# Row-by-row indirect DMAs of a graph network: straight-line GpSimd code that reads whole tables

## Chip, cores, metric

One Trainium2 chip, one core. The metric is the device time of one execution in microseconds (us).

## What is computed

Two graph layers on 6250 nodes of 128 features and 100000 edges (src, dst), each with a residual and a layer norm:

```python
# layer 0: attention along the edges, softmax over the edges of one src
scores = sum(q[src] * k[dest], -1) / sqrt(D) + attention_mask
weights = softmax of scores within each src
out = segment_sum(v[src] * weights, dest) @ Wo.T + bo
x = layernorm(x + out)
# layer 1: a two-layer MLP on each edge, summed by src, then an MLP on the nodes
h = silu(concat([x[src], x[dst], edge_attr_2]) @ eW1 + eb1)
agg = segment_sum(silu(h @ eW2 + eb2), src)
x = layernorm(x + silu(concat([x, agg]) @ nW1 + nb1) @ nW2 + nb2)
```

## The kernel before

An edge is a record of 16 floats: 8 attention biases, 2 attributes, dst, the lane of src within its window of 128 nodes, its id. The program runs through stages, each a block with one instruction stream per engine and a barrier at its end.

**Placing** (`place_and_project`, L362). The 784 columns of 128 records are taken 8 at a time (98 groups, `PG`). VectorE, TensorE and ScalarE work out for each record the row of `records_dram` where it belongs, sorted by window. VectorE ends a group with the row indices `row_idx` (L499), in a buffer of two groups; it first waits until the DMAs of two groups ago have landed. GpSimd copies each column of records into `rec_out` (L627) and scatters it with an indirect DMA, 128 rows of 64 bytes (L640); the copy of a column is issued ahead of the DMA of the column before. 784 copies, 784 DMAs. Beside it q, k and v are projected, 49 windows.

**Loading** (`load_records`, L688). The sorted records, 832 columns, come back into SBUF as `records`, in 7 pieces; VectorE takes the lanes out of each (L717).

**Scoring** (`score`, L742). 104 groups of 8 columns. GpSimd casts each column's whole record to integers (`sc_idx`, L789), and then gathers 128 rows of k by its dst (L800): 832 casts, 832 DMAs, in a ring of 4 groups. TensorE makes the q rows with one-hot matrices; VectorE multiplies and sums.

**Softmax**, **weighing** (`weigh`, L1063 on; 832 scatters that add, L1106) and the **middle** of the network follow.

**Edges** (`edges`, L1630). 208 groups of 4 columns. VectorE casts the dst of a group to `ed_idx` (L1694, three groups ahead) once that ring slot's gather before has landed; GpSimd gathers 4 times 128 rows of `b_rows_dram` (L1685) in a ring of 4 groups; TensorE sums window rows, attributes and gathered rows in PSUM (`ps_z`), and a SiLU, a second matmul, a SiLU and a one-hot matmul follow; VectorE adds the sums to `vals` (L1719). **Finale**: the MLP on nodes.

GpSimd's three loops are written with `each_pair` and `each_group`: some groups at either end as straight-line code, the rest in a hardware loop of 2 or 4 groups. The order on every queue is the program's order; nothing schedules it.

Of the kernel before, what the change touches and what calls it, by code (L numbers as in the profile page):

```python
# [26 lines left out]
F32 = mybir.dt.float32  # L27
BF16 = mybir.dt.bfloat16
I32 = mybir.dt.int32

P = 128
# [8 lines left out]
ET = 784  # L40
LASTE = E - (P - 1) * ET
G = 4
# [3 lines left out]
R = 16  # L46
# [12 lines left out]
PG = 8  # L59
IT = ET // PG  # L60
RF = NT // 16

# [299 lines left out]
def place_and_project(c, e, a):  # L362
# [6 lines left out]
             "place_counted place_slots masked slot slot_int slot_tile slot_scaled slot_lane slot_chunk slot_line row_index rec_slot")  # L369
    (s_ohl, s_ohw, s_tr, s_lt, s_gram, s_gm, s_tab, s_hist, s_slots, s_msk, s_red, s_int, s_tile, s_mul, s_lane, s_chunk,  # L370
     s_line, s_idx, s_rec) = semaphores(nc, c.sems, names)
    s_sent = semaphores(nc, c.stack, "records_sent0 records_sent1")
# [3 lines left out]
    with ExitStack() as t:  # L376
# [15 lines left out]
        idx = sb("row_idx", [P, 2, PG], I32)  # L392
        out = sb("rec_out", [P, 2, PG, R], F32)
# [12 lines left out]
        with nc.Block() as block:  # L406
# [28 lines left out]
            def _(dve):  # L435
# [37 lines left out]
                def finish(i, b):  # L473
# [24 lines left out]
                    wait_count(dve, s_sent[b], 16 * PG * i)  # L498
                    dve.scalar_tensor_tensor(out=idx[:, b, :], in0=chunk[:, :], scalar=-float(NT - 1), in1=line[:, :],  # L499
# [122 lines left out]
            @block.gpsimd  # L622
            def _(pool):
                pool.wait_ge(c.s_rfill, 16 * (NT // RF))

                def record(g, b, j):
                    pool.tensor_copy(out[:, b, j, :], e.rec[:, bass.ds(g * PG + j, 1), :].rearrange("p t r -> p (t r)")  # L627
                                     ).then_inc(s_rec, 1)

                def send(i, b):  # L630
                    g = 2 * i + b
                    wait_count(pool, s_sent[b], 16 * PG * i)
                    record(g, b, 0)
                    pool.wait_ge(s_idx, g + 1)
                    for j in range(PG):
                        if j + 1 < PG:
                            record(g, b, j + 1)
                        pool.wait_ge(s_rec, PG * g + j + 1)
                        pool.sem_inc(s_turn, 1)
                        pool.indirect_dma_start(  # L640
                            c.rec_rows, bass.IndirectOffsetOnAxis(ap=idx[:, b, j:j + 1], axis=0),
                            out[:, b, j, :], None, bounds_check=SLOTS - 1, oob_is_err=False).then_inc(s_sent[b], 16)
                each_pair(pool, send)
                for b in range(2):
                    pool.wait_ge(s_sent[b], 16 * PG * (IT // 2))
# [42 lines left out]
def load_records(c):  # L688
# [6 lines left out]
    s_l, s_t, s_row, s_out = semaphores(nc, c.sems, "lanes_taken lanes_turned lane_rows lanes_out")  # L695
# [46 lines left out]
def score(c):  # L742

    nc = c.nc
    names = ("sc_onehot_t sc_q sc_index sc_prod sc_dot sc_score sc_line sc_kept sc_ids sc_ids_t "
             "sc_ids_kept sc_ids_shift sc_steps")
    (s_oht, s_q, s_idx, s_prod, s_dot, s_sc, s_line, s_kept, s_ids, s_idt, s_idk, s_shift,
# [9 lines left out]
    with ExitStack() as t:  # L757
# [3 lines left out]
        idx = sb("sc_idx", [P, RING, SG, R], I32)  # L761
# [10 lines left out]
        with nc.Block() as block:  # L772
# [8 lines left out]
            def _(pool):  # L781
# [4 lines left out]
                def index(g, r, k):  # L786
                    if k == 0:
                        wait_count(pool, s_k[r], (g - r) * (16 * SG // RING))
                    pool.tensor_copy(idx[:, r, k, :], c.rec[:, bass.ds(g * SG + k, 1), :].rearrange("p t r -> p (t r)")  # L789
                                     ).then_inc(s_idx, 1)  # L790

                def gather(g, r):
                    wait_count(pool, s_prod, g - RING + 1)
                    for k in range(SG):
                        ahead, slot, there = (g, r, True) if k + 1 < SG else group_at(g, r, 1, NS)
# [1309 lines left out]
```

## Time and profile before

| what | us |
|---|---|
| median of 3 runs (5821.47 to 5829.13) | 5822.44 |
| span of the profiled execution, first to last instruction | 5485.4 |
| placing, first to last of GpSimd's DMAs | 160.33 to 1328.12 |
| scoring, the same | 1362.57 to 2517.35 |
| edges, the same | 4350.84 to 5412.71 |

The profile carries no time of its own for the profiled execution, only its span. It lies 337.0 us under the median of the runs; that much is spent before the first and after the last instruction of the record. Engines: PE is TensorE, PEld its weight load, DVE VectorE, ACT ScalarE, POOL GpSimd, SP SyncE. An indirect DMA on POOL (DMA_INDIRECT) is busy while GpSimd makes its descriptors; the data moves after that on the DMA engines. "Idle" before an instruction is the time its engine did nothing just before it, with what ended that; "issue" is time in which nothing that the profile shows was waited for.

### The profile page before, as it was taken

The numbers are of one execution on the slowest core, as the hardware profiler recorded it, in microseconds if no ns is written. First come the engines' busy times: TensorE is split into PE (matmuls) and PEld (weight loads), VectorE is DVE, ScalarE is ACT, GpSimd is POOL, SyncE is SP. The second block draws the span as 40 slices with busy tenths as digits, with TensorE's granted clock in tenths as the row PEclk, the third lists the DMA queues.
The fourth block names the chain that finished last, engine by engine and source line by source line (L and its number), as shares of the span: only waits on it lengthen the run. The fifth ranks groups of instructions, "written<-read, shape, count | busy, mean of one in ns | idle before, by whom it ended". The sixth has DMA issues, their size and how long they took to land. (4 is left out here: it accounts for less than half of the span.)

```text
span 5485.4 us, 85482 instructions
## 1 busy us (share of the span) xinstructions
PE 2866.4 (52%) x21791; PEld 2562.0 (47%) x21792; DVE 2423.9 (44%) x6521; ACT 779.2 (14%) x1649; POOL 4120.0 (75%) x5002
## 2 busy tenths in 40 slices
PE   6444444442333333331565666666653577778776
PEld 5333333331333333331455555555553466677765
DVE  7655555552333333336533333333333644444445
ACT  0111111110000000000111111111111322222222
POOL 1688888886888888883588888888886377777773
PEclk9666666665555555555787778787786799999999
DMA  2300000001222222220243444444445433333333
GB/s 85 110 11 11 10 11 11 11 10 68 72 72 71 69 72 70 70 71 21 24 35 35 35 35 35 35 35 35 35 35 94 120 78 77 77 78 76 78 76 82
DMA packets 301449, 293.46 MB, mean 53 GB/s; under 512 B 62976, under 2 KB 240570, under 8 KB 300377
## 3 DMA queue, kind: packets, MB, share of 16 engines
q0 software_dynamic: 201376, 176.66, 20.7%
q1 hardware_dynamic: 100024, 116.22, 7.2%
q8 instruction: 22, 0.36, 0.0%
q14 instruction: 27, 0.22, 0.0%
HBM read 198.74 MB, written 93.92 MB: 53 GB/s over the span
## 5 line engine op out<-in xcount | busy, mean ns | idle before, releaser
L1106 POOL DMA_INDIRECT sums_dram<-we_merged_rows,we_idx x832 | 1289.7, 1550 | 385.3 <-issue 204.6
L1685 POOL DMA_INDIRECT ed_bg<-b_rows_dram,ed_idx x832 | 808.7, 972 | 262.5 <-issue 240.7
L800 POOL DMA_INDIRECT sc_k<-k_rows_dram,sc_idx x832 | 827.1, 994 | 145.3 <-POOL sc_idx L789 130.4
L640 POOL DMA_INDIRECT records_dram<-rec_out,row_idx x784 | 779.2, 994 | 207.9 <-POOL rec_out L627 164.4
L900 PE MATMUL ps_q<-tab,sc_oht 128*128 x1664 | 386.5, 426 | 740.8 <-DVE sc_oht L813 740.8
L900 PEld LDWEIGHTS ps_q<-tab,sc_oht 128*128 128x128 f32 x1664 | 358.8, 327 | 772.3 <-issue 772.3
L1257 PE MATMUL ps_merged<-we_rows,we_same_dst 128*128 128x129 f32 x1664 | 337.7, 366 | 585.2 <-issue 428.9
L1257 PEld LDWEIGHTS ps_merged<-we_rows,we_same_dst 128*128 128x128 f32 x1664 | 288.9, 261 | 620.9 <-issue 611.4
L1159 DVE SCALAR_TENSOR_TENSOR we_firsts<-we_merged_rows,lane_unmark,two_marks 128x4 f32<-128x4 f32 x208 | 46.3, 222 | 1012.6 <-ACT we_merged_rows L1202 1012.6
L828 DVE TENSOR_TENSOR sc_prods<-ps_q,sc_k 128x1024 f32<-128x1024 f32 x104 | 127.3, 1224 | 745.3 <-DMA sc_k<-k_rows_dram,sc_idx 745.3
L1719 DVE TENSOR_TENSOR vals<-vals,ps_ed_s 128x128 f32 x832 | 238.9, 287 | 391.8 <-PE ps_ed_s L1816 296.7
L1795 PE MATMUL ps_z<-ident,ed_bg 128*128 128x128 f32 x832 | 250.2, 301 | 243.7 <-DMA ed_bg<-b_rows_dram,ed_idx 243.5
L591 PE MATMUL ps_table<-place_ohw,place_oh 128*128 128x400 bf16 (+7 forms) x784 | 167.4, 392 | 323.2 <-DVE place_ohw L216 323.2
L1237 PE MATMUL ps_dst_row<-ident,we_dsts 128*128 128x128 f32 x1664 | 329.7, 365 | 0.0
L1237 PEld LDWEIGHTS ps_dst_row<-ident,we_dsts 128*128 128x128 f32 x1664 | 315.2, 282 | 0.0
L1202 ACT ACTIVATE we_merged_rows<-ps_merged 128x516 f32<-128x516 f32 x208 | 125.0, 601 | 1283.1 <-DMA sums_dram<-we_merged_rows,we_idx 1268.8
L1792 PE MATMUL ps_z<-ed_oht,tab 128*128 128x128 bf16 x2496 | 306.1, 226 | 0.0
L591 PEld LDWEIGHTS ps_table<-place_ohw,place_oh 128*128 128x128 bf16 x784 | 113.6, 163 | 381.8 <-issue 329.6
L627 POOL COPY rec_out<-records 128x16 f32 (+1 forms) x784 | 182.6, 243 | 129.3 <-POOLq L276 112.1
L1247 PE MATMUL ps_v<-value_tab,we_oht 128*128 x1664 | 275.1, 317 | 0.1
L572 PE MATMUL ps_place_t<-identb,place_oh 128*128 128x128 bf16 x784 | 92.0, 283 | 313.4 <-DVE place_oh L222 313.4
L1795 PEld LDWEIGHTS ps_z<-ident,ed_bg 128*128 128x128 f32 x832 | 121.6, 146 | 276.9 <-DMA ed_bg<-b_rows_dram,ed_idx 276.6
(307 smaller groups left out, 6534.6 us busy)
## 6 DMA issues: line engine op xcount, KB each, us to landing
sc_lane_rows<-lanes_dram SPq DMA_DIRECT2D x104, 256.0 KB, 3.4
ed_lane_rows<-lanes_dram SPq DMA_DIRECT2D x104, 256.0 KB
sc_k<-k_rows_dram,sc_idx POOLq DMA_INDIRECT x832, 2.5
sums_dram<-we_merged_rows,we_idx POOLq DMA_INDIRECT x832, 3.3
ed_bg<-b_rows_dram,ed_idx POOLq DMA_INDIRECT x832
sums_dram<-zero_rows SPq DMA_DIRECT2D x20, 640.0 KB, 8.7
records_dram<-rec_out,row_idx POOLq DMA_INDIRECT x784
mi_rows<-sums_dram SPq DMA_DIRECT2D x48, 256.0 KB, 4.5
```

Source lines behind the costliest of these rows:

```text
L591: ins = pe.matmul(table[:, k:PG, :], ohl[:, b, :, k], ohw[:, b, k, :].unsqueeze(1).to_broadcast([P, PG - k, WC]), start=(k == 0), stop=Tru ...
L640: pool.indirect_dma_start(c.rec_rows, bass.IndirectOffsetOnAxis(ap=idx[:, b, j:j + 1], axis=0), out[:, b, j, :], None, bounds_check=SLOTS ...
L800: pool.indirect_dma_start(kg[:, r, k * F:(k + 1) * F], None, c.k_dram[:, :], bass.IndirectOffsetOnAxis(ap=idx[:, r, k, C_DST:C_DST + 1], a ...
L900: ins = pe.matmul(psq[b][:, k * F:(k + 1) * F], oht[:, b, k, :], c.qtab[:, bass.ds(win[k] * F, F)], start=True, stop=True)
L1106: pool.indirect_dma_start(c.acc_dram[k][:, :], bass.IndirectOffsetOnAxis(ap=idx[:, r, k:k + 1], axis=0), rows[:, r, k, 0:F], None, compute ...
L1237: ins = pe.matmul(psd[:, k * P:(k + 1) * P], dst[:, r, k:k + 1].to_broadcast([P, P]), c.ident[:, :], start=True, stop=True)
L1247: ins = pe.matmul(psv[b][:, k * F:(k + 1) * F], oht[:, b, k, :], c.vtab[:, bass.ds(win[k] * F, F)], start=True, stop=True)
L1257: ins = pe.matmul(merged[b][:, k, 0:F + 1], same[:, b, k, :], con[:, b, k, :], start=True, stop=True)
L1685: pool.indirect_dma_start(bg[:, r, k * F:(k + 1) * F], None, c.b_dram[:, :], bass.IndirectOffsetOnAxis(ap=idx[:, r, k:k + 1], axis=0)).the ...
L1719: dve.tensor_tensor(acc, acc, pss[r % 2][:, k * P:(k + 1) * P], ALU.add).then_inc(s_add, 1)
L1792: pe.matmul(z, c.tab[:, j, bass.ds(win[k] * F, F)], oht[:, r, k, :], start=False, stop=False)
L1795: ins = pe.matmul(z, bg[:, r, k * F:(k + 1) * F], c.ident[:, :], start=False, stop=True, is_transpose=True)
```

## The change

GpSimd's three streams become straight-line code without loops, one DMA per column. In placing the DMA reads its 128 records straight from `records` (no `rec_out`, no copy), and the indices from a table of all 784 columns; VectorE no longer waits before it writes indices, and GpSimd waits for its own DMAs of four groups ago (`AHEAD`). The table `dst_index` of all 832 columns is filled in `load_records` by seven more casts on VectorE; scoring and edges take their indices from it (no `sc_idx`, no `ed_idx`, no casts in the stages). In edges the one-hot `ed_ohf` moves onto the records' memory to make room, and VectorE runs two groups ahead in place of three.

```diff
 place_and_project
-        idx = sb("row_idx", [P, 2, PG], I32)
-        out = sb("rec_out", [P, 2, PG, R], F32)
+        idx = sb("row_idx", [P, ET], I32)
...
-                    wait_count(dve, s_sent[b], 16 * PG * i)
-                    dve.scalar_tensor_tensor(out=idx[:, b, :], in0=chunk[:, :], scalar=-float(NT - 1), in1=line[:, :],
+                    dve.scalar_tensor_tensor(out=idx[:, bass.ds(g * PG, PG)], in0=chunk[:, :], scalar=-float(NT - 1), in1=line[:, :],
...
-                def record(g, b, j):
-                    pool.tensor_copy(out[:, b, j, :], e.rec[:, bass.ds(g * PG + j, 1), :].rearrange("p t r -> p (t r)")
-                                     ).then_inc(s_rec, 1)
-                def send(i, b):
-                    g = 2 * i + b
-                    wait_count(pool, s_sent[b], 16 * PG * i)
-                    record(g, b, 0)
-                    pool.wait_ge(s_idx, g + 1)
-                    for j in range(PG):
-                        if j + 1 < PG:
-                            record(g, b, j + 1)
-                        pool.wait_ge(s_rec, PG * g + j + 1)
...
+                for g in range(IT):
+                    pool.wait_ge(s_idx, g + 1)
+                    wait_count(pool, s_sent[g % AHEAD], 16 * PG * (g // AHEAD))
+                    pool.sem_inc(s_turn, 1)
+                    for t in range(g * PG, (g + 1) * PG):
+                        pool.indirect_dma_start(
+                            c.rec_rows, bass.IndirectOffsetOnAxis(ap=idx[:, t:t + 1], axis=0),
+                            e.rec[:, t, :], None, bounds_check=SLOTS - 1, oob_is_err=False).then_inc(s_sent[g % AHEAD], 16)
 load_records
+                    dve.tensor_copy(c.didx[:, t0:t0 + n], c.rec[:, t0:t0 + n, C_DST]).then_inc(s_di, 1)
 score
-                    pool.tensor_copy(idx[:, r, k, :], c.rec[:, bass.ds(g * SG + k, 1), :].rearrange("p t r -> p (t r)")
-                                     ).then_inc(s_idx, 1)
...
+                for g in range(NS):
+                    r = g % RING
                     wait_count(pool, s_prod, g - RING + 1)
+                    pool.sem_inc(s_turn, 1)
                     for k in range(SG):
+                        t = g * SG + k
                         pool.indirect_dma_start(kg[:, r, k * F:(k + 1) * F], None, c.k_dram[:, :],
-                                                bass.IndirectOffsetOnAxis(ap=idx[:, r, k, C_DST:C_DST + 1], axis=0)
+                                                bass.IndirectOffsetOnAxis(ap=c.didx[:, t:t + 1], axis=0)
                                                 ).then_inc(s_k[r], 16)
 edges
-        ohf = sb("ed_ohf", [P, RING, G, P], F32)
+        ohf = c.rec[:, 0:RING * G * P // R, :].rearrange("p t r -> p (t r)").rearrange("p (b k n) -> p b k n", b=RING, k=G)
...
-                def gather(g, r):
-                    pool.wait_ge(s_idx, g + 1)
+                for g in range(NG):
+                    r = g % RING
                     wait_count(pool, s_z, g - RING + 1)
                     pool.sem_inc(s_turn, 1)
                     for k in range(G):
+                        t = g * G + k
                         pool.indirect_dma_start(bg[:, r, k * F:(k + 1) * F], None, c.b_dram[:, :],
-                                                bass.IndirectOffsetOnAxis(ap=idx[:, r, k:k + 1], axis=0)
+                                                bass.IndirectOffsetOnAxis(ap=c.didx[:, t:t + 1], axis=0)
                                                 ).then_inc(s_b[r], 16)
...
-                def index(g, r):
-                    wait_count(dve, s_b[r], (g - r) * (16 * G // RING))
-                    dve.tensor_copy(idx[:, r, :], c.rec[:, bass.ds(g * G, G), C_DST]).then_inc(s_idx, 1)
...
-                    for by, work in ((3, index), (2, front), (0, by_edges), (-3, back)):
+                    for by, work in ((2, front), (0, by_edges), (-3, back)):
...
-                each_group(dve, step, lead=3, lag=3, rings=2)
+                each_group(dve, step, lead=2, lag=3, rings=2)
```

How GpSimd's queue stands in placing, before; one group of 8 columns in the loop, up to the next group's first copy. A row is one instruction, or xN of a kind; `waits` names the semaphores it waits for (`rec_slot` is the copy's, `records_sent0` and `1` the DMAs').

```order
L627 ISA [waits records_sent0]
L627 COPY rec_out<-records 128x16
L634 REGISTER_ALU
L627 ISA [waits row_index]
L627 COPY rec_out<-records 128x16
L640 DMA records_dram<-rec_out,row_idx 106496x16 [waits rec_slot]
L627 ISA
L627 COPY rec_out<-records 128x16
L640 DMA records_dram<-rec_out,row_idx 106496x16 [waits rec_slot]
```

And of the change, two groups of 8:

```order
L630 DMA records_dram<-records,row_idx 106496x16 [waits row_index,records_sent0]
L630 DMA records_dram<-records,row_idx 106496x16 x7
L630 DMA records_dram<-records,row_idx 106496x16 [waits row_index,records_sent1]
L630 DMA records_dram<-records,row_idx 106496x16 x7
```

Every copy between two DMAs is gone, and one DMA in eight waits for anything. Scoring, before, on the same queue:

```order
L800 DMA sc_k<-k_rows_dram,sc_idx 128x128 [waits sc_index]
L789 CAST sc_idx<-records 128x16
L800 DMA sc_k<-k_rows_dram,sc_idx 128x128 [waits sc_index]
```

And of the change:

```order
L781 DMA sc_k<-k_rows_dram,dst_index 128x128 [waits sc_prod]
L781 DMA sc_k<-k_rows_dram,dst_index 128x128 x7
```

The cast ahead of each gather is gone; the wait for the product of four groups ago stays, once in a group.

## Rows read from the trace of the kernel before

**Rows 1.** the page of the whole program: busy time, share and instructions of each engine

```profile
PE 2866.4 (52%) x21791; PEld 2562.0 (47%) x21792; DVE 2423.9 (44%) x6521; ACT 779.2 (14%) x1649; POOL 4120.0 (75%) x5002
```

**Rows 2.** busy time by stage: placing, scoring, edges. Columns stand in the first line

```profile
core 0: us, PE busy (x) PEld busy (x) DVE busy (x) ACT busy (x) POOL busy (x), PEclk, DMA share, GB/s
159.00:1328.00 1169.00, 478.41 (x4779) 376.88 (x4779) 629.68 (x1649) 128.33 (x243) 958.24 (x1567) 0.62 0.07 19
1361.00:2518.00 1157.00, 405.39 (x1766) 373.66 (x1766) 409.22 (x766) 33.16 (x152) 1007.78 (x1667) 0.58 0.28 71
4351.00:5413.00 1062.00, 819.70 (x7844) 738.37 (x7845) 487.42 (x1643) 282.37 (x621) 808.50 (x832) 0.97 0.32 77
```

**Rows 3.** groups by line on GpSimd: line, operation, count | busy us, mean ns | idle

```profile
L800 POOL DMA_INDIRECT sc_k<-k_rows_dram,sc_idx x832 | 827.1, 994 | 145.3 <-POOL sc_idx L789 130.4 <-issue 15.0
L1685 POOL DMA_INDIRECT ed_bg<-b_rows_dram,ed_idx x832 | 808.7, 972 | 262.5 <-issue 240.7 <-DVE ed_idx L1694 17.5 <-PE ps_z L1795 4.3
L640 POOL DMA_INDIRECT records_dram<-rec_out,row_idx x784 | 779.2, 994 | 207.9 <-POOL rec_out L627 164.4 <-issue 43.5
L627 POOL COPY rec_out<-records 128x16 f32 (+1 forms) x784 | 182.6, 243 | 129.3 <-POOLq L276 112.1 <-DVE row_idx L499 16.4
L789 POOL CAST sc_idx<-records 128x16 int32 (+1 forms) x832 | 181.0, 218 | 3.2
```

**Rows 4.** GpSimd in order of time, placing: start us, us, instruction [idle before <-releaser]

```profile
160.33 1.34 POOL L640 DMA_INDIRECT records_dram<-rec_out,row_idx  x1 [0.69 <-POOL rec_out L627]
...
604.80 0.21 POOL L627 COPY rec_out<-records 128x16 f32 x1
605.17 0.98 POOL L640 DMA_INDIRECT records_dram<-rec_out,row_idx  x1 [0.16 <-POOL rec_out L627]
...
613.21 0.97 POOL L640 DMA_INDIRECT records_dram<-rec_out,row_idx  x1 [0.30 <-issue]
...
1327.15 0.97 POOL L640 DMA_INDIRECT records_dram<-rec_out,row_idx  x1 [0.30 <-issue]
```

**Rows 5.** GpSimd in order of time, scoring

```profile
1362.57 1.01 POOL L800 DMA_INDIRECT sc_k<-k_rows_dram,sc_idx  x1 [0.77 <-POOL sc_idx L789]
...
2515.15 0.96 POOL L800 DMA_INDIRECT sc_k<-k_rows_dram,sc_idx  x1 [0.16 <-POOL sc_idx L789]
2516.41 0.94 POOL L800 DMA_INDIRECT sc_k<-k_rows_dram,sc_idx  x1 [0.30 <-issue]
```

**Rows 6.** GpSimd in order of time, edges

```profile
4341.48 0.12 POOL L1678 MEMSET ed_attrs<- 128x12 bf16 x1
4350.84 1.22 POOL L1685 DMA_INDIRECT ed_bg<-b_rows_dram,ed_idx  x1 [9.24 <-DVE ed_idx L1694]
...
4400.26 0.95 POOL L1685 DMA_INDIRECT ed_bg<-b_rows_dram,ed_idx  x1 [0.30 <-PE ps_z L1795]
...
5411.77 0.94 POOL L1685 DMA_INDIRECT ed_bg<-b_rows_dram,ed_idx  x1 [0.30 <-issue]
```

**Rows 7.** VectorE in order of time, placing

```profile
173.61 0.17 DVE L499 SCALAR_TENSOR_TENSOR row_idx<-slot_chunk_i,slot_line_f 128x8 int32<-128x8 int32 x1
...
180.28 0.17 DVE L499 SCALAR_TENSOR_TENSOR row_idx<-slot_chunk_i,slot_line_f 128x8 int32<-128x8 int32 x1
...
603.92 0.17 DVE L499 SCALAR_TENSOR_TENSOR row_idx<-slot_chunk_i,slot_line_f 128x8 int32<-128x8 int32 x1 [4.56 <-DMA records_dram<-rec_out,row_idx]
```

**Rows 8.** the scatter's line alone: count, duration ns min/median/max, first and last start

```profile
L640 POOL DMA_INDIRECT records_dram<-rec_out,row_idx x784: 966/977/1402, 160.3 to 1327.1; - x196
```

**Rows 9.** waits in edges, 4400 to 5350 us: us in total, times, longest us

```profile
PE ps_z L1795 <- DMA ed_bg<-b_rows_dram,ed_idx: 212.3, 161, 2.4
```

**Rows 10.** VectorE in order of time, loading of the records

```profile
1346.76 0.27 DVE L717 CAST lanes<-records 128x128 bf16<-128x128 f32 x1 [2.23 <-DMA records<-records_dram]
```

**Rows 11.** the page, DMA queues that carry instructions: packets, MB, share of 16 engines

```profile
q8 instruction: 22, 0.36, 0.0%
q14 instruction: 27, 0.22, 0.0%
```

More of the change, by code:

```diff
@@ L61 @@
 RF = NT // 16
+AHEAD = 4
 class Ctx:
@@ L368, in place_and_project @@
     names = ("place_onehot_n place_onehot_w place_turned place_onehot_t place_gram place_earlier place_table_kept "
-             "place_counted place_slots masked slot slot_int slot_tile slot_scaled slot_lane slot_chunk slot_line row_index rec_slot")
+             "place_counted place_slots masked slot slot_int slot_tile slot_scaled slot_lane slot_chunk slot_line row_index")
     (s_ohl, s_ohw, s_tr, s_lt, s_gram, s_gm, s_tab, s_hist, s_slots, s_msk, s_red, s_int, s_tile, s_mul, s_lane, s_chunk,
-     s_line, s_idx, s_rec) = semaphores(nc, c.sems, names)
-    s_sent = semaphores(nc, c.stack, "records_sent0 records_sent1")
+     s_line, s_idx) = semaphores(nc, c.sems, names)
+    s_sent = semaphores(nc, c.stack, " ".join(f"records_sent{n}" for n in range(AHEAD)))
     (s_turn,) = semaphores(nc, c.sems, "scatter_turn")
@@ L624, in _ @@
                 pool.wait_ge(c.s_rfill, 16 * (NT // RF))
[L626 to L645 removed]
+                for g in range(IT):
+                    pool.wait_ge(s_idx, g + 1)
+                    wait_count(pool, s_sent[g % AHEAD], 16 * PG * (g // AHEAD))
+                    pool.sem_inc(s_turn, 1)
+                    for t in range(g * PG, (g + 1) * PG):
+                        pool.indirect_dma_start(
+                            c.rec_rows, bass.IndirectOffsetOnAxis(ap=idx[:, t:t + 1], axis=0),
+                            e.rec[:, t, :], None, bounds_check=SLOTS - 1, oob_is_err=False).then_inc(s_sent[g % AHEAD], 16)
+                for n in range(AHEAD):
+                    pool.wait_ge(s_sent[n], 16 * PG * len(range(n, IT, AHEAD)))
 NG = NT // G
@@ L784, in _ @@
                 pool.memset(c.trail[:, :, :], -BIG).then_inc(s_init, 1)
-                def index(g, r, k):
-                    if k == 0:
-                        wait_count(pool, s_k[r], (g - r) * (16 * SG // RING))
-                    pool.tensor_copy(idx[:, r, k, :], c.rec[:, bass.ds(g * SG + k, 1), :].rearrange("p t r -> p (t r)")
-                                     ).then_inc(s_idx, 1)
-                def gather(g, r):
+                for g in range(NS):
+                    r = g % RING
                     wait_count(pool, s_prod, g - RING + 1)
+                    pool.sem_inc(s_turn, 1)
                     for k in range(SG):
-                        ahead, slot, there = (g, r, True) if k + 1 < SG else group_at(g, r, 1, NS)
-                        if there:
-                            index(ahead, slot, (k + 1) % SG)
-                        pool.wait_ge(s_idx, SG * g + k + 1)
-                        pool.sem_inc(s_turn, 1)
+                        t = g * SG + k
                         pool.indirect_dma_start(kg[:, r, k * F:(k + 1) * F], None, c.k_dram[:, :],
-                                                bass.IndirectOffsetOnAxis(ap=idx[:, r, k, C_DST:C_DST + 1], axis=0)
+                                                bass.IndirectOffsetOnAxis(ap=c.didx[:, t:t + 1], axis=0)
                                                 ).then_inc(s_k[r], 16)
-                index(0, 0, 0)
-                each_group(pool, gather, groups=NS)
             @block.vector
```

15 lines of the change are left out of this document (6 added, 9 removed).

## The prediction

> **What bounds the kernel now.** I read the page first: GpSimd is busy 75% of the span, more than any other engine [rows 1]. A share of the whole says little, so the second view was the busy time by stage [rows 2]. In placing, scoring and edges GpSimd is busy 958, 1008 and 809 us of 1169, 1157 and 1062; VectorE has 630, 409 and 487, TensorE 478, 405 and 820. Only TensorE in edges comes near, and there it waits 212 us of 950 for GpSimd's gathers [rows 9]. So three GpSimd streams set the length of three stages, and the question is what one DMA costs in each of them.
>
> The third view is GpSimd in order of time. In placing the first scatter starts at 160.33 and the last ends at 1327.15 + 0.97 = 1328.12 [rows 4]: 1167.8 us for 784, 1.490 us each. Scoring runs from 1362.57 to 2516.41 + 0.94 = 2517.35 [rows 5]: 1154.8 for 832, 1.388 each. Edges runs from 4350.84 to 5411.77 + 0.94 = 5412.71 [rows 6]: 1061.9 for 832, 1.276 each. Edges has no copies on GpSimd, and is the pattern that the other two are turned into.
>
> The reader should look at the idle time ahead of a DMA. After a copy it is 0.16 us; after another DMA it is 0.30, put down to issue, in placing [rows 4], in scoring [rows 5] and in edges [rows 6]. A copy of 0.21 us between two DMAs thus does not cost 0.21: it takes 0.21 + 0.16 = 0.37 where two DMAs in a row have 0.30. Most of it lies in a gap that is there anyway.
>
> **Placing.** What the removed copies free is read per DMA. After the change a DMA costs its own time plus 0.30. Its own time is 0.994 in the mean now [rows 3]; one that follows a DMA takes 0.97 where one that follows a copy takes 0.98 [rows 4], so I take off 0.01. The copies have a mean of 0.243 [rows 3] where an undisturbed one takes 0.21 [rows 4]; some of these 0.03 us of disturbance will meet DMAs instead. I take a third, 0.01. That makes 0.994 + 0.30 = 1.294 us. The bounds are 0.97 + 0.30 = 1.27 with no disturbance at all, and 1.294 + 0.03 = 1.324.
>
> The wait that moves: VectorE now waits 4 to 5 us in each group until the scatters of two groups ago have landed [rows 7], and this goes. What is late next? VectorE must give an index group each 8 x 1.294 = 10.4 us. Two index groups with no wait between them are 180.28 - 173.61 = 6.67 us apart [rows 7], so it will run ahead and finish long before GpSimd does. Only the start is bound by it: group 1 has its indices at 173.78, when group 0 (8 DMAs from about 160) is already out. From 174.0 on GpSimd has 776 DMAs x 1.294 = 1004.1 us: the end comes at 1178.1 in place of 1328.1, **150.0 us less**. The new wait for the scatters of four groups ago costs nothing: these were issued 30 us before. The seven casts added in loading fall into waits of 2.23 us for the next piece [rows 10]; each is about as long as the 0.27 of its neighbour. Nothing for them.
>
> **Scoring.** Here a cast of 0.218 in the mean [rows 3] and a gap of 0.16 become one gap of 0.30. The DMA's own 0.994 [rows 3] loses 0.013 to 0.02 (0.96 after a cast, 0.94 after a DMA [rows 5]); I take 0.013, add a third of the casts' disturbance, 0.004, and get 1.285. 832 of them are 1069.1 us, against 1154.8: 85.7, and 0.5 at the start, where the 0.77 us for the first cast go [rows 5]. **86.2 us less**. VectorE's 409 us and TensorE's 405 [rows 2] leave them far from taking over. Bounds: 0.945 + 0.30 = 1.245 (119 us less) and 0.994 + 0.30 + 0.013 = 1.307 (67 less).
>
> **Edges.** There is no copy on GpSimd to take out. The casts were on VectorE, which is not the bound. GpSimd's gap is 0.30 even where it had to wait for TensorE's `ps_z` [rows 6], and also in the last groups, which were straight-line code already [rows 6]. Taking the loop away gives nothing there. What goes is the first wait: GpSimd is ready at 4341.60 and starts at 4350.84, after VectorE's first `ed_idx`, 9.24 us [rows 6]. With the table it can start at once and has four groups in its ring before TensorE must take any away. **8.9 us less**, with 0.3 left as the gap. Bounds: 0, if TensorE's later start holds back the fifth group, and 8.9 + 832 x 0.027 = 31, if the mean of 0.972 [rows 3] falls to 0.945.
>
> **Sum.** 150.0 + 86.2 + 8.9 = 245.1 us. The span 5485.4 would be 5240; the 337.0 us around it (median minus span) I leave as they are, so 5822.4 - 245.1 = **5577 us**. The bounds together: 169 + 119 + 31 = 319 less (5503), and 127 + 67 + 0 = 194 less (5628).
>
> **Rivals.** *A: VectorE without its wait holds GpSimd back.* VectorE, now paced, will work without a break for some 98 x 6.67 = 654 us, about 505 of the 784 scatters. The scatter's durations are 966/977/1402 ns [rows 8]: something delays some of them by up to 0.43 us. If each of these 505 lost half of that, 0.21, it would be 106 us, and 5683. Against it: VectorE is busy 54% of placing already [rows 2], and the mean stands only 17 ns over the median [rows 3, 8]; the same VectorE work in less time should hit as often in all.
> The Trainium skill (SBUF — State Buffer, SBUF: two separate sides) speaks for A: a VectorE instruction in a two-port mode locks GpSimd out of a shared port for its whole length, and an indirect DMA cannot write descriptors meanwhile. By that rule alone most scatters beside a busy VectorE would be late; the few 17 ns of the mean do not bear this out as a large cost.
>
> *B: VectorE and TensorE do not keep up without the wait.* If an index group took as long as now (1.490 x 8 = 11.9 us), placing would keep its time: 5577 + 150 = 5727. Against it: the 6.67 us.
>
> *C: straight-line code is slower to issue, and the kernel gets slower.* GpSimd ran 64 + 64 + 32 = 160 of its 2448 DMAs in these stages outside loops (8 groups of each); now all. Each must be fetched once. The place is the GpSimd stream, the price a stall per stretch of code. It decides from 245 / 2448 = 0.10 us per DMA; at 0.13, it would be +318, 5895, slower. For it: the two instruction queues now carry 49 packets and 0.58 MB in all, little of it for these loops [rows 11]. Against it: the straight-line tails of all three stages have the same 0.30 as the loops [rows 4 to 6]. The Trainium skill (Runtime: NRT & Kernel Launch, Instruction fetch mechanics) is against it too: fetch is sequential, runs ahead and is mostly hidden, and a taken branch is what costs; no run here shows that yet.
>
> *D: the gap of 0.30 belongs to waits and register work, and falls to 0.15 in straight-line code.* 2448 x 0.15 = 367 more, 5210. Against it: the same tails.
>
> *E: the change doesn't do what it says*, for instance the DMA from the large table costs more than from the packed copy, so that placing gains nothing but its gaps. At +0.1 us on 784: 5577 + 78 = 5655.
>
> **Chances.** Forecast 0.80, A 0.06, B 0.03, C 0.03, D 0.02, E 0.06. The range takes the bounds of the sum, cut where all terms would have to lie at one end (5503 to 5535), and reaches up past 5628 towards E: 5535 to 5645. About 0.2% is what a measurement of this kernel can tell from no change, 11.6 us. Faster by more than that are all cases but C, less 0.01 for a mix of A and C that nearly cancels the gain: 0.96; same 0.01; slower 0.03.
>
> **What would show it.** In the profile after: no copies or casts on GpSimd; the scatter's line with a mean near 0.994 and a gap of 0.30; placing from 160 to about 1178, VectorE silent for its last 300 to 350 us; scoring near 1069 us; edges as long as before but started 9 us earlier. Wrong would be: scatters whose mean rises above 1.05 while VectorE is busy (A); GpSimd waiting for `row_idx` beyond the first groups (B); gaps above 0.30, or long ones at regular distances (C); gaps well under 0.30 (D).

## The result and the profile after

The change takes 5953.25 us (median of 4 runs, 5944.42 to 5956.85), the kernel before 5824.23 (4 runs, 5821.47 to 5829.13). The ratio is 1.0219, 95% interval 1.0205 to 1.0233: **slower by 129 us**, where 5577 and a gain of 245 were forecast. The profiled execution is one of these, 5953.02 us with a span of 5951.1, so 1.9 us lie around the span.

First the page of the changed kernel, and its busy time by stage. The columns are those of [rows 2].

```profile
PE 2911.2 (49%) x21791; PEld 2589.8 (44%) x21792; DVE 2370.5 (40%) x6320; ACT 769.3 (13%) x1649; POOL 3742.2 (63%) x3386
```

```profile
159.00:1466.00 1307.00, 513.00 (x4779) 388.35 (x4779) 621.53 (x1646) 126.88 (x243) 802.43 (x784) 0.59 0.07 17
1499.00:2717.00 1218.00, 333.23 (x1732) 301.92 (x1732) 400.77 (x747) 33.69 (x146) 796.40 (x832) 0.61 0.27 67
4555.00:5874.00 1319.00, 890.08 (x7774) 814.98 (x7774) 446.56 (x1439) 269.34 (x614) 799.11 (x832) 0.84 0.25 62
```

GpSimd's busy time fell from the 4120.0 us of [rows 1] to 3742.2, as meant. But no stage is shorter: placing has 1307 us for the 1169 of [rows 2], scoring 1218 for 1157, edges 1319 for 1062. Next, the groups by line on GpSimd (line, operation, count | busy us, mean ns | idle ahead of it):

```profile
L630 POOL DMA_INDIRECT records_dram<-records,row_idx x784 | 802.4, 1024 | 631.1 <-DVE row_idx L498 393.4 <-issue 237.7
L1664 POOL DMA_INDIRECT ed_bg<-b_rows_dram,dst_index x832 | 799.1, 960 | 519.3 <-remote 230.1 <-issue 222.6 <-PE ps_z L1769 66.6
L781 POOL DMA_INDIRECT sc_k<-k_rows_dram,dst_index x832 | 796.4, 957 | 421.2 <-issue 244.9 <-DVE sc_prods L807 176.4
```

The gap between two DMAs was forecast rightly or nearly so: 237.7 / 749 = 0.32 us in placing, 0.30 in scoring (244.9 / 803), by the number of waits that the record puts down to issue. What is new is that GpSimd is no longer what the stages wait for. In placing it waits 393.4 us for VectorE's indices (127.2 of them before the first scatter), in scoring 176.4 for VectorE's products, in edges 230.1 for a releaser that the records put down to "remote": a semaphore rises that no recorded instruction raised just then. The waits of VectorE say more. These are those of the change in placing (us in total, times, longest us):

```profile
DVE place_table L453 <- remote: 246.5, 28, 13.8
DVE place_masked L476 <- remote: 174.2, 51, 11.4
DVE place_earlier L468 <- remote: 96.2, 31, 7.9
```

All three instructions read what TensorE's matmuls wrote. The first profile of the kernel before had none of this in placing; its one large wait on VectorE there was the landing of its scatters:

```profile
DVE row_idx L499 <- DMA records_dram<-rec_out,row_idx: 450.6, 93, 9.0
```

One group of the change's placing in order of time shows the shape of it (start us, us, instruction [idle before <-releaser]); the lines between are left out:

```profile
613.62 0.20 PE L602 MATMUL ps_slots<-place_table_parts,place_oh_t 128*128 128x50 bf16 x1 [1.10 <-issue]
...
614.35 0.26 PE L571 MATMUL ps_place_t<-identb,place_oh 128*128 128x128 bf16 x1 [0.48 <-issue]
...
616.48 0.58 PE L571 MATMUL ps_place_t<-identb,place_oh 128*128 128x128 bf16 x4 [1.09 <-issue]
...
617.93 0.37 PE L571 MATMUL ps_place_t<-identb,place_oh 128*128 128x128 bf16 x2 [0.86 <-issue]
...
623.16 0.97 POOL L630 DMA_INDIRECT records_dram<-records,row_idx  x1 [0.31 <-issue]
626.52 0.57 DVE L476 TENSOR_TENSOR place_masked<-ps_slots,place_ohw 128x400 f32<-128x400 f32 x1 [7.20 <-remote]
626.61 1.02 ACT L537 ACTIVATE place_oh_t<-ps_place_t 128x1024 bf16<-128x1024 bf16 x1 [16.12 <-remote]
...
628.27 1.71 PE L590 MATMUL ps_table<-place_ohw,place_oh 128*128 128x400 bf16 x8 [9.97 <-DVE place_ohw L217]
...
629.72 0.17 DVE L498 SCALAR_TENSOR_TENSOR row_idx<-slot_chunk_i,slot_line_f 128x8 int32 x1 [0.21 <-DVE slot_line_f L494]
...
630.77 1.11 POOL L630 DMA_INDIRECT records_dram<-records,row_idx  x1 [6.63 <-DVE row_idx L498]
```

TensorE issues single transposes with gaps of 0.5 to 1.1 us. Its last matmul of `ps_slots` ends at 613.9 and that of `ps_place_t` at 618.3, yet VectorE and ScalarE start on them only at 626.5, **8 us after the later of the two**. VectorE itself was not what was late: `place_masked` waits for one semaphore, which only the matmuls of `ps_slots` raise, and in the trace it rises at 626.50. (The record models the ends of matmuls, so whether the work or only its signal came late can't be told from it.) GpSimd's last scatter of the streak ended at 624.13. So the two were released 2.4 us after the stream of scatters had stopped. Then VectorE needs 3.2 us for its indices, GpSimd stands idle for 6.63, and it starts again. I call this "late completions" below.

### The profile page after: what moved, and what is told of

Same layout as the page of the kernel before. It is cut to its first block and busy times, and to the rows that moved or that the text cites. A ratio compares the mean times of both kernels' runs of the same rounds, so it can differ in the third digit from the quotient of the medians.

```text
span 5951.1 us, 79482 instructions
## 1 busy us (share of the span) xinstructions
PE 2911.2 (49%) x21791; PEld 2589.8 (44%) x21792; DVE 2370.5 (40%) x6320; ACT 769.3 (13%) x1649; POOL 3742.2 (63%) x3386
## 2 busy tenths in 40 slices
DMA packets 301471, 293.64 MB, mean 49 GB/s; under 512 B 62976, under 2 KB 240570, under 8 KB 300377
## 5 line engine op out<-in xcount | busy, mean ns | idle before, releaser
L630 POOL DMA_INDIRECT records_dram<-records,row_idx x784 | 802.4, 1024 | 631.1 <-DVE row_idx L498 393.4
L1664 POOL DMA_INDIRECT ed_bg<-b_rows_dram,dst_index x832 | 799.1, 960 | 519.3 <-remote 230.1
L781 POOL DMA_INDIRECT sc_k<-k_rows_dram,dst_index x832 | 796.4, 957 | 421.2 <-issue 244.9
L879 PE MATMUL ps_q<-tab,sc_oht 128*128 x1664 | 313.0, 365 | 794.7 <-DVE sc_oht L792 539.2
L879 PEld LDWEIGHTS ps_q<-tab,sc_oht 128*128 128x128 f32 x1664 | 292.5, 274 | 820.6 <-issue 820.5
L1790 PE MATMUL ps_ed_s<-records,ed_efs 128*128 128x128 f32 x1664 | 288.4, 328 | 335.2 <-ACT ed_efs L1736 221.2
L807 DVE TENSOR_TENSOR sc_prods<-ps_q,sc_k 128x1024 f32<-128x1024 f32 x104 | 127.2, 1223 | 764.7 <-remote 724.7
L1790 PEld LDWEIGHTS ps_ed_s<-records,ed_efs 128*128 128x128 f32 x1664 | 253.4, 233 | 360.5 <-issue 331.7
L590 PE MATMUL ps_table<-place_ohw,place_oh 128*128 128x400 bf16 (+7 forms) x784 | 155.4, 370 | 379.8 <-DVE place_ohw L217 276.2
L1780 PEld LDWEIGHTS ps_ed_o<-w,ed_hts 128*128 128x128 f32 x1664 | 266.6, 226 | 31.4 <-issue 16.5
L1780 PE MATMUL ps_ed_o<-w,ed_hts 128*128 128x128 f32 x1664 | 265.0, 308 | 13.7 <-issue 13.7
```

The costliest lines, as they stand in the source:

```text
L590: ins = pe.matmul(table[:, k:PG, :], ohl[:, b, :, k], ohw[:, b, k, :].unsqueeze(1).to_broadcast([P, PG - k, WC]), start=(k == 0), stop=Tru ...
L630: pool.indirect_dma_start(c.rec_rows, bass.IndirectOffsetOnAxis(ap=idx[:, t:t + 1], axis=0), e.rec[:, t, :], None, bounds_check=SLOTS - 1, ...
L781: pool.indirect_dma_start(kg[:, r, k * F:(k + 1) * F], None, c.k_dram[:, :], bass.IndirectOffsetOnAxis(ap=c.didx[:, t:t + 1], axis=0)).the ...
L879: ins = pe.matmul(psq[b][:, k * F:(k + 1) * F], oht[:, b, k, :], c.qtab[:, bass.ds(win[k] * F, F)], start=True, stop=True)
L1664: pool.indirect_dma_start(bg[:, r, k * F:(k + 1) * F], None, c.b_dram[:, :], bass.IndirectOffsetOnAxis(ap=c.didx[:, t:t + 1], axis=0)).the ...
L1780: ins = pe.matmul(pso[b][:, k * F:(k + 1) * F], ht[:, b, k * P:(k + 1) * P], w2[:, :], start=False, stop=(k == G - 1))
```

## Where the rows before came from

The profiled execution of the kernel before has a span of 5485.4 us; its timed runs have a median of 5822. The prediction, and the section on the time before it, took these 337 us for something around the span. Around the span of the change lie 1.9. This suggests that the profiled execution was of another kind than the timed ones, and the first thing to try was the kernel before again, with its three parts of the change one by one.

**Experiment 1: the kernel before once more.** No edit.

> The kernel before, unchanged, for a second profile beside its runs. The profiled span of 5485.4 us lies 337 us under its median, that of the change only 1.9 us under its own. Theory 1 (the first profile of before caught an execution without the late TensorE completions that the change shows): a span near 5820 here, edges near 1300 us in place of 1062, with waits put down to remote. Theory 2 (337 us really lie outside the span of this kernel): span near 5485 again, and 5820 as the time.

5895.99 us as the median; the profiled execution took 5895.01 with a span of 5893.3, so 1.7 us lie around it. On this chip the kernel before has a median of 5891.31. The busy time by stage of this run:

```profile
159.00:1386.00 1227.00, 500.44 (x4779) 386.91 (x4779) 632.05 (x1647) 127.16 (x243) 968.90 (x1567) 0.59 0.07 18
1420.00:2636.00 1216.00, 380.48 (x1766) 349.18 (x1766) 410.80 (x766) 34.25 (x149) 1006.96 (x1666) 0.59 0.26 67
4465.00:5815.00 1350.00, 888.76 (x7787) 805.91 (x7787) 476.55 (x1652) 269.58 (x616) 802.97 (x832) 0.82 0.24 60
```

Counted from GpSimd's first DMA of the stage to its last, placing has 58 us more than in the first profile, scoring 60 and edges 282, with the same code and nearly the same busy times. The waits of VectorE in placing say why: of the 450.6 us for landings 158.8 are left, and "remote" has come in.

```profile
DVE place_masked L476 <- remote: 198.5, 56, 8.7
DVE row_idx L499 <- DMA records_dram<-rec_out,row_idx: 158.8, 43, 6.2
DVE place_table L453 <- remote: 92.4, 21, 16.2
```

The kernel before has late completions too, in this execution, whose time is that of its timed runs. The first profile had caught an execution without them; no later profile of a kernel with these DMAs so close did, and why that one had none stays open.

The clock that TensorE was granted is a second difference. In placing it hardly differs (0.62 of full speed in the mean in the first profile, 0.59 here), but in edges it is 0.97 against 0.82, and TensorE's busy time there 819.7 against 888.8 us. No run separates the two in edges: the lower clock can follow from the late completions, or add to the stage by itself. The 69 us of busy time are the smaller part of the 282. The lengths of the stages (first to last DMA of GpSimd, us) in all runs:

| run | time | before, same chip | ratio, 95% | placing | scoring | edges |
|---|---|---|---|---|---|---|
| before, first profile | - | 5824.23 | - | 1168 | 1155 | 1062 |
| the change | 5953.25 | 5824.23 | 1.0219 (1.0205 to 1.0233) | 1306 | 1217 | 1318 |
| before again | 5895.99 | 5891.31 | 1.0006 (0.9993 to 1.0019) | 1226 | 1215 | 1344 |
| placing alone | 6012.15 | 5891.31 | 1.0194 (1.0164 to 1.0223) | 1339 | 1220 | 1341 |
| scoring alone | 5900.04 | 5891.31 | 1.0017 (1.0005 to 1.0029) | 1205 | 1221 | 1344 |
| edges alone | 5880.06 | 5891.31 | 0.998 (0.9968 to 0.9993) | 1225 | 1218 | 1335 |
| spaced, 128 columns | 5847.48 | 5825.04 | 1.0046 (1.0035 to 1.0057) | 1215 | 1201 | 1316 |
| spaced, 192 | 5866.17 | 5893.41 | 0.9946 (0.9927 to 0.9966) | 1232 | 1208 | 1330 |
| spaced, 256 | 5854.36 | 5893.41 | 0.993 (0.9912 to 0.9947) | 1188 | 1240 | 1327 |
| spaced, 384 | 5985.93 | 5825.04 | 1.0277 (1.0248 to 1.0307) | 1252 | 1329 | 1308 |
| one pause per group | 5868.65 | 5893.41 | 0.9959 (0.9944 to 0.9975) | 1210 | 1222 | 1327 |
| 256 in placing, 128 in scoring | 5811.64 | 5820.78 | 0.9982 (0.9973 to 0.9991) | 1187 | 1205 | 1319 |

Rows with nearly the same time for the kernel before compare directly. That time differs between chips by 70 us, so times and stage lengths don't compare across rows where that figure differs much, and ratios only roughly: how the 70 us lie by stage, and whether the other kernels have them too, no run shows. The weighing stage has 1542 or 1543 us in all of these.

## The parts alone

**Experiments 2 to 4.** Each is the kernel before with one function of the change: `place_and_project` (the table of row indices, no copies, four landings ahead); `score`, with the index table that loading fills (edges keeps its loops, but copies its indices from that table and has its one-hot on the records' memory); `edges`, with the same table.

> The kernel before with placing alone changed (straight line, no copies, whole table). Theory 1, TensorE's completions come late wherever GpSimd sends DMAs without a copy between them: placing takes about 1306 us as in the change, against 1168 before, so the time rises by about 138. Rival, the loss needs all of the change (one long straight-line program): placing near 1010 us, the time falls by 150.

> Scoring alone changed, with the index table; placing as before, edges with the loops of before but its VectorE index copies taken from the table. Theory 1: scoring 1217 us against 1155, the time rises by about 62. Rival: scoring near 1070, the time falls by 86.

> Edges alone changed, with the index table and the one-hot on the records' memory. If GpSimd's back-to-back stream is the cause, edges was such a stream before too (no copies on GpSimd): about 1318 us in both kernels, so this run is within 20 us of before (5822). Rival, straight-line code is what does it: edges rises from 1062 to 1318, and the time with it by some 250 us.

Placing alone costs 1.9%: nearly the whole loss. Its stage goes from 1226 to 1339 us. The waits of VectorE there:

```profile
DVE place_masked L476 <- remote: 412.7, 52, 16.1
DVE place_earlier L468 <- remote: 117.5, 47, 5.7
DVE place_table L453 <- remote: 81.6, 41, 5.8
```

And GpSimd, where it starts again after a wait:

```profile
615.95 1.11 POOL L630 DMA_INDIRECT records_dram<-records,row_idx  x1 [6.71 <-DVE row_idx L498]
...
643.37 1.11 POOL L630 DMA_INDIRECT records_dram<-records,row_idx  x1 [6.60 <-DVE row_idx L498]
```

A cycle of 27.4 us for two groups: 16 scatters x 1.28 = 20.5, then 6.6 idle. That is 1.71 us per scatter in place of 1.27. Scoring alone gives nothing: GpSimd now waits 180.0 us for VectorE's products, and the stage keeps its length (1221 us for 1215). The 62 us more that were expected had been reckoned from the first profile, and 9 came. Edges alone gives 0.2%, 11 us, about the 8.9 of the prediction, though the stage is now bound elsewhere.

## Is it TensorE and VectorE themselves, or the scatters beside them?

**Experiment 5: no scatters.** The change without placing's scatters; GpSimd only raises the semaphore. The records never reach their rows, so scoring and edges work on fill values, and only placing is read.

```diff
-                    for t in range(g * PG, (g + 1) * PG):
-                        pool.indirect_dma_start(...).then_inc(s_sent[g % AHEAD], 16)
+                    pool.sem_inc(s_sent[g % AHEAD], 16 * PG)
```

> The change with the 784 scatters of placing left out, so the records that later stages read are the fill values; read for placing alone. Theory A: TensorE and VectorE without GpSimd's DMAs run at their own 6.67 us per group, placing ends about 98 x 6.67 = 654 us after its first indices, near 815 us. Rival, TensorE is held back by something of its own (its instruction stream, its clock): placing stays above 1000 us.

VectorE's last `row_idx` of placing comes 684 us after the first, 7.0 per group, near the 6.67 that the prediction read [rows 7]; no wait of placing is put down to remote. TensorE and VectorE can do it in 684. Two more runs ask which part of a scatter holds them up.

**Experiment 6: GpSimd busy, but with no DMA.** Each scatter is a memset of 0.8 us; again only placing is read.

```diff
-                        pool.indirect_dma_start(...).then_inc(s_sent[g % AHEAD], 16)
+                        wait_count(pool, s_pace, t)
+                        pool.memset(c.didx[:, :], 0).then_inc(s_pace, 1)
+                        pool.sem_inc(s_sent[g % AHEAD], 16)
```

> The change with each scatter of placing replaced by a memset of GpSimd over the 832 columns of the index table (about 0.81 us, back to back): GpSimd is as busy as before but starts no DMA. The records never reach their rows, so scoring and edges work on fill values and only placing is read. If a busy GpSimd as such (its port, its semaphores) makes TensorE's completions late, placing shows waits put down to remote and lasts well over 1000 us. If it is its DMAs, there are none and the stage runs at the pace of GpSimd's memsets, 784 x about 0.95 = 745 to 800 us.

**Experiment 7: scatters that write nothing.** All indices out of bounds: each DMA is issued and worked out, and no record is written. Only placing is read.

```diff
+                pool.memset(c.didx[:, :], 2 * SLOTS).then_inc(s_pace, 1)
+                pool.wait_ge(s_pace, 1)
...
-                            c.rec_rows, bass.IndirectOffsetOnAxis(ap=idx[:, t:t + 1], axis=0),
+                            c.rec_rows, bass.IndirectOffsetOnAxis(ap=c.didx[:, t:t + 1], axis=0),
```

> The change with placing's scatters given indices that all lie out of bounds, so that each DMA is issued and its descriptors are worked out, but no record is written; scoring and edges again work on fill values and only placing is read. If what makes TensorE's completions late is the writing of descriptors, or their traffic, placing falls to GpSimd's own pace, 784 x 1.27 = 996 us plus a start of 15. If the issue of the DMAs on GpSimd alone does it, placing stays near the change's 1306.

With memsets, the stage is GpSimd's alone. Its line, and the largest waits of VectorE in placing:

```profile
L632 POOL MEMSET dst_index<- x784: 791/792/929, 159.3 to 951.0; 128x832 int32 x196
```

```profile
DVE place_oh L223 <- issue: 20.1, 45, 0.5
DVE row_idx L499 <- DVE slot_line_f L495: 19.3, 90, 0.2
```

792 us, with a memset every 1.01 us, and nothing late. With scatters that write nothing, placing lasts 1303 us, as the change's 1306, and the late completions are all there:

```profile
DVE place_table L454 <- remote: 250.2, 27, 15.8
DVE place_masked L477 <- remote: 142.2, 48, 11.4
DVE place_earlier L469 <- remote: 131.8, 33, 8.0
```

The traffic of placing falls from 10 to 5 GB/s there and makes no difference. So in placing neither a busy GpSimd nor the records written make TensorE's completions late, but the stream of indirect DMAs as such (each is a single execution, but 684 and 792 us against 1303 lie far beyond the noise). Whether it is the descriptors that GpSimd writes or their being worked off by the queues isn't told apart: the number of packets of the whole program (301471) is the same in both.

## Does the distance between the DMAs matter?

**Experiments 8 and 9: a memset ahead of each DMA**, over 128 or 384 columns, in placing, scoring and edges. The DMAs are then 1.35 and 1.57 us apart in place of 1.27 (here placing with 128):

```diff
                     for t in range(g * PG, (g + 1) * PG):
+                        wait_count(pool, s_pace, t)
+                        pool.memset(c.didx[:, 0:128], 0).then_inc(s_pace, 1)
                         pool.indirect_dma_start(
```

> The change, with a memset of 128 columns on GpSimd ahead of every indirect DMA of placing, scoring and edges (about 0.2 us; with the gap of 0.16 it makes DMAs 1.33 us apart in place of 1.27). Theory A, TensorE's completions come late when GpSimd's DMAs follow each other directly and fast: placing falls from 1306 us to about 1226, edges from 1318 to 1215 to 1250, scoring stays near 1217; the time falls by 100 to 150 from the change's 5950. Rival, spacing has nothing to do with it: each stage stays or grows by 0.06 us per DMA, some 50 us each.

> The same with a memset of about 384 columns, DMAs some 1.58 us apart. Theory A: the late completions are gone, and each stage is only its DMAs: placing about 784 x 1.58 = 1239 us, scoring and edges about 1315 each, no waits put down to remote. Rival, lateness independent of spacing: placing above 1400 and edges above 1450.

**Adding work to GpSimd ahead of every DMA makes the change faster**: 1.0046 of the kernel before with 128 columns, where the change has 1.0219, both on chips where the kernel before takes 5824 to 5825. Placing goes from 1306 to 1215; edges, where 1215 to 1250 were expected, stays at 1316. With 384 columns no wait of any engine is put down to remote any more, but now GpSimd's own stream is the bound, with 1.60 us per DMA in the mean in placing and scoring and 1.57 in edges, and the time is 5985.93.

In edges of that run VectorE waits for a recorded matmul, TensorE's last, as it did in the first profile, and TensorE for the gathers:

```profile
DVE vals L1702 <- PE ps_ed_s L1799: 556.8, 157, 7.9
```

```profile
PE ps_z L1778 <- DMA ed_bg<-b_rows_dram,dst_index: 387.4, 186, 4.0
```

**Experiments 10 and 11: 192 and 256 columns**, 1.41 and 1.46 us apart.

> The change with a memset of GpSimd over 192 columns ahead of each of its DMAs in placing, scoring and edges; the DMAs should then stand 1.41 us apart (memset about 0.28, gap 0.16, DMA 0.97), between the 1.35 and the 1.57 of the two spaced kernels before it. THEORY (TensorE's completions arrive late beside a dense stream of GpSimd's DMAs, a spacing removes it): the optimum lies between the two; less lateness than at 1.35. Placing 784 x 1.41 plus 30 to 60 us = 1140 to 1200, scoring 832 x 1.40 plus 20 = 1185 to 1210, edges between the two bounds 816 x 1.40 = 1142 and the 1316 measured at 1.33: 1200 to 1290. Time 5700 to 5830. RIVAL (the gain at 1.35 was from something else than the spacing, for instance the one missing write of a busy port, and every added us is lost): placing 1215 + 784 x 0.055 = 1258, scoring 1201 + 46 = 1247, edges 1316 + 46: time about 5960.

> The same with 256 columns, DMAs 1.47 us apart. THEORY: nearly no completion late, stages near their count of DMAs: placing 784 x 1.47 = 1152 plus 20, scoring 832 x 1.46 = 1215 plus 10, edges 832 x 1.44 = 1198 plus 10. Time 5984 - 80 (placing) - 104 (scoring) - 100 (edges) = about 5700. RIVAL: only the 1.57 us have no lateness, by a threshold between; then the waits put down to remote stay as at 1.35, and the time is above 5850.

**Experiment 12: one pause per group**, about as long in all as 256 columns ahead of each DMA, and the DMAs of a group 1.27 us apart again:

```diff
                 for g in range(IT):
+                    for n in range(2):
+                        wait_count(pool, s_pace, 2 * g + n)
+                        pool.memset(c.didx[:, :], 0).then_inc(s_pace, 1)
                     pool.wait_ge(s_idx, g + 1)
```

> The same mean distance of 1.47 us, but as one pause of GpSimd per group (1.7 us ahead of 8 DMAs in placing and scoring, 0.95 us ahead of 4 in edges), the DMAs within a group 1.27 us apart as in the change. If what counts is a backlog that grows with the number of DMAs in a row, and a pause drains it, stage lengths come out as at 256 columns (about 5700). If each DMA holds something back for a time of its own and TensorE falls behind inside each streak, placing stays near the change's 1306 and edges near 1318, and the time is about 5900 to 5960.

Both expectations of a clear best spacing missed: about 5700 was expected from 256 columns, 5854 came, and 5866 from 192, where 5700 to 5830 were expected. Placing with 256 did nearly as expected (1188 for 1172; VectorE's remote waits fall from the change's 517 us to 289, and GpSimd waits 3.8 for an index after the start). In experiment 14, with the same placing, they are 47 us and the stage has 1187: this sum varies between executions and isn't what sets the length there. With 192 columns placing has 1232, above the 1140 to 1200 expected and above the 1215 of 128; those stand on different chips, so whether 192 is worse isn't shown. Scoring with 256 has no remote wait left and is GpSimd's alone, 832 x 1.49 = 1240. **Edges did not move**: 1316, 1330 and 1327 us at 1.35, 1.41 and 1.46, with 580.5 us of remote waits on `vals` at 256 columns, and only at 1.57 do they vanish. With gathers 1.25 us apart (the median) edges had them in each of experiments 1 to 4, and none in the first profile. So a distance that is enough in one stage is not in another; what a stage of its own adds to it stays open.

The pause per group came out like the even spacing in edges (1327 each) and in scoring a little shorter (1222 for 1240), and within 22 us in placing (1210 for 1188). At 5868.65 us it lies between its two expectations, nearer to the even spacing's 5854 that was measured. This speaks against an effect of each pair of DMAs by itself, and for short rests working off what has been held back (VectorE's remote waits in placing are 189 us there). That agrees with the timeline above, where the two completions came 2.4 us after the streak of 24 scatters ended. But the mean distance over a stage doesn't decide alone: the edges of the change have 1318 / 832 = 1.58 us per gather with their halts, and many late completions, where an even 1.57 had none.

**Experiment 13: does the weighing stage lack late completions because no other queue runs there?** Its DMAs are 1.85 us apart (1542 / 832). SyncE was given loads of 256 KB there:

```diff
+                for g in range(0, NG, 2):
+                    wait_count(sp, s_oht, g)
+                    wait_count(sp, s_spare, 16 * (g // 2))
+                    sp.dma_start(spare[:, :], lanes_of(c, g * G, 2 * G)).then_inc(s_spare, 16)
```

> The change with one extra 256 KB load per two groups issued by SyncE in weighing, the one stage of scatters that has no SyncE DMAs and no late completions (1541 us in every profile). Theory B, the lateness needs SyncE's DMAs beside GpSimd's: weighing grows by 50 us or more, with waits put down to remote. Theory A (only the spacing of GpSimd's DMAs matters, 1.85 us here): weighing stays within 10 us of 1541.

5944.25 us, weighing 1542 as ever: SyncE's loads are not what is missing there. Its DMAs lie beyond the 1.57 us at which no other stage had late completions; that this is the reason isn't tested.

**Experiment 14: the best spacing of each stage together**, 256 columns in placing, 128 in scoring, none in edges.

> The change with the spacing that each stage did best with: 256 columns ahead of each DMA in placing (1188 us there), 128 columns in scoring (1201), none in edges (1318). Sum against the change's profiled 5951: -118 - 16 + 0 = about 5817. Against the kernel before on the same chip: its three stages together 1226 + 1215 + 1344 = 3785, here 3707, so 78 less (ratio 0.987) where the kernel before runs at 5893; on a chip where it runs at 5825, no change within 0.3%. If the stages hand their lateness on (what is saved in placing is lost in edges), the time is 5850 to 5870, ratio above 0.993.

5811.64 us, ratio 0.9982 (0.9973 to 0.9991): faster than the change by over 2%, and than the kernel before by 0.2%, whose copy or cast ahead of each DMA is replaced by a memset and index tables. Whether it is the best isn't shown: 256 columns in all three stages had the lower ratio, 0.993, on a chip where the kernel before takes 5893, and has no run on one like this. The stages came as expected (1187, 1205, 1319), so what is saved in placing isn't lost in edges.

## Why the prediction was wrong

**The step that failed** is the first reading, "So three GpSimd streams set the length of three stages". In executions like the timed ones late completions of TensorE share in setting that length, so taking work off GpSimd freed nothing, and in placing the denser scatters made them worse: VectorE's waits put down to remote there are 327 us in experiment 1 and 612 in experiment 2. Two terms of the sum rest on it. Placing was to be 150.0 us shorter; changed alone it came out about 113 us longer (1226 to 1339, experiments 1 and 2). Scoring was to be 86.2 shorter; changed alone it kept its length (1215 and 1221).

The sign of it was there before: "the 337.0 us around it (median minus span) I leave as they are". Nothing of that size lies around a span; it is 1.7 to 2.1 us in every run since, and what is said ahead of the prediction, that they are spent before the first and after the last instruction, is wrong too. A second profile of the same kernel, before any change, is longer than the first by 58 us in placing, 60 in scoring and 282 in edges. (That is on a chip where it takes 70 us more; how the 5824 lie by stage on the first has no profile.) The change's span is longer than that of the first profile by 5951.1 - 5485.4 = 466 us: 138 in placing, 62 in scoring, 256 in edges and 10 elsewhere.

**What a DMA costs** was nearly right. Forecast were 1.294 us in placing and 1.285 in scoring; after, it is 1.024 + 0.32 = 1.34 in placing, just above the bound of 1.324, and 0.957 + 0.305 = 1.26 in scoring, inside its bounds. GpSimd's busy time fell by 378 us. Nothing of it reached the time.

**"It will run ahead and finish long before GpSimd does"** failed, with the rows that it rested on. The 6.67 us between two index groups [rows 7] came from the first profile, with the scatters paced by the copies and no completion late. Beside scatters 1.27 us apart a group takes 1306 / 98 = 13.3 us in the change and 1339 / 98 = 13.7 in experiment 2; without scatters it is 7.0. Rival B had this effect ("as long as now", 5727) and not its cause or size: what was taken for the engines' own pace depends on what GpSimd does beside them. The wait for landings in the kernel before also reads differently now: of its 450.6 us 158.8 are left in experiment 1, beside 327 of waits put down to remote on VectorE.

**Scoring**, -86.2: the stage has 1215 us in experiment 1, 1217 in the change. VectorE's products wait 702.5 us in 46 waits put down to remote in the change, where the first profile has 736.6 for the gathers themselves. In experiment 1 VectorE has 482 us of remote waits there already: the bound had moved before the change was made.

**Edges**, -8.9: 0.2% in experiment 4, of the size forecast; the bounds 0 to 31 hold it.

**Rival A** looked for the disturbance between other engines: VectorE holding up GpSimd's DMAs, by a shared port. The trace of after has a scatter of 1024 ns for 994, 24 us over 784, while its stages lost far more. The rule of the Trainium skill on the port lock (SBUF — State Buffer, SBUF: two separate sides) is about VectorE and GpSimd, and doesn't cover what the runs show, that TensorE's completions come late beside GpSimd's DMAs. **Rival C** gave a time 58 us from the truth for a wrong reason. Straight-line code showed no slower issue: the gap is 0.30 in scoring (244.9 / 803), and the one queue that grew carries little:

```profile
q14 instruction: 49, 0.40, 0.0%
```

22 packets more than in [rows 11], over 5951 us. The Trainium skill's rule that fetch runs ahead and is mostly hidden (Runtime: NRT & Kernel Launch, Instruction fetch mechanics) agrees with that. **D** fell with the same gap; **E** too, as the DMA from the large table is no dearer (0.957 for 0.994 in scoring).

## What to carry to other kernels

Before a row is used, put the profile's span beside the timed median: where they differ by far more than is usual (here by 337 us for 1.7 to 2.1), the rows are of another execution than the one that is to be made faster, and a second profile is worth more than any reading of the first. An engine that issues one thing after another can be too fast for its neighbours: here the copies between GpSimd's scatters were part of the spacing that kept TensorE's completions from coming later still, and a memset of 0.2 to 0.3 us in their place did the same work. When a stream is made denser, ask who else's completions it travels beside, and try it with idle time put back in.

## What the runs showed of the hardware

- In placing, completions of TensorE reached VectorE and ScalarE late, by 8 us in the group shown, while GpSimd issued indirect DMAs 1.27 us apart, and TensorE's own issue had gaps of 0.5 to 1.1 us meanwhile. None was late beside memsets 1.01 us apart, and beside DMAs that wrote nothing VectorE's waits put down to remote were 524 us, as the change's 517. Through which path this goes, and whether the matmuls or only their signals are late, no run shows.
- At 1.55 to 1.57 us apart it was gone in all three stages. At 1.44 to 1.46 it was gone in scoring, cost little in placing, and in edges as much as at 1.34.
- A GpSimd instruction between two indirect DMAs hides in the gap between them in part: the gap is 0.30 us DMA to DMA and 0.16 to 0.17 after a memset, so 0.22 us of memset costs 0.08 to 0.09.
- The kernel before ran once, in a profile, with a span of 5485 us, and has medians of 5821 to 5896 in all timings, some 70 us apart from chip to chip.
